# Three front stages made one, and the bf16 remainders of two attention projections formed in PSUM

## The chip, the cores and the metric

The kernel runs on one core of a Trainium2 chip. The metric is the device time of one execution in microseconds (us). A core has five engines that run side by side and meet at semaphores: TensorE (PE, matrix products into PSUM; its weight loads are listed as PEld), VectorE (DVE), ScalarE (ACT), GpSimd (POOL) and SyncE (SP, which here issues nearly all DMAs).

## The reference, cut to what matters

The reference is a stack of eleven layers on x of 2048 tokens (2 sequences of 1024) by 128 features, all in float32. The change touches the first four layers and the two attentions of the last block.

```python
x = x + 0.5 * ffn0(layernorm(x))     # the coupling net, three cycles
x = x + scan(layernorm(x))           # diagonal linear recurrence
x = x + 0.5 * ffn0(layernorm(x))     # the coupling net again
x = x + 0.5 * ffn1(layernorm(x))     # top-1 of 7 experts, and a shared expert
...
# ffn0: gf = global_net(mean over the tokens of a sequence)
for _ in range(3):
    tf = sigmoid(gelu(gelu(gelu(out @ w1) @ w2) @ w3) @ w4)
    combined = 0.7 * gf + 0.3 * tf
    out = out + (0.1 + range * (combined - 0.5) * 2) * twist(out)
# scan: h_t = A * h_(t-1) + (x_t @ B.T + b);  y = h @ C.T + c
# last block: x + attention_g(rmsnorm(x)), then x + attention_l(rmsnorm(x)),
# where q and k of each head are rotated (rope) and divided by their root mean square
```

## The kernel before

x lies in SBUF as 16 tiles of 128 tokens by 128 features; four tiles are a chunk of 512 tokens, and there are four chunks. The kernel is a row of seventeen stages. Each stage is a block with one program for each engine, written out by hand in its order, and ends in a barrier of all engines (`close` in `Core.block`, line 116).

The front is three such stages: `coupling_stage` (c1_), `scan_stage` (s_) and `coupling_stage` again (c2_). Each begins with `LayerNorm`: DVE takes the statistics of a chunk (L170, L173), GpSimd raises the variance to -0.5 (L195, L197), DVE normalises (L180), TensorE turns four tiles to features by tokens (L206) and ScalarE copies them to xnT (L212). In a coupling stage there follow three cycles. In one, TensorE's layers 1 to 4 (L438, L444, L452, L459) alternate with ScalarE's three gelus and a tanh (L506, L510, L514, L519); SP swaps the two halves of the features by DMA (L373, L374); DVE adds the base part of the output (L411), then for each chunk forms a product with the gate (L414) and adds it (L417). In the first cycle the base waits for the global net (L434, L496 to L501), and that for the sums over a sequence (L398). At the end TensorE turns the output back (L483) and DVE joins it to x (L421). The scan stage multiplies by B (L589), adds a bias on ScalarE (L575), runs the recurrence on DVE (L607) and multiplies by C (L582).

After the front stands `top1_stage` (m1_), whose argument `ahead` says how many chunks come already normalised (none here). It loads the shared expert's weights at its start (L695); TensorE turns, makes logits (L770) and runs the shared expert (L787, L792). It is called a second time later (m2_) with three chunks ahead.

`gqa_project_stage` is called for the global (gp_) and the local (lp_) attention of the last block. TensorE projects four tiles a chunk (L3198), DVE multiplies by rope's table (L3301) and sums (L3318), ScalarE squares (L3271), DVE takes means (L3322) and, after ScalarE's root (L3275), scales the heads (L3334); TensorE turns queries (L3207) and keys (L3214). Then the float32 result is split in three bf16 parts by `Split`: ScalarE rounds a part (L1517 from the remainder), DVE subtracts it from the remainder in SBUF (L1525), twice. The parts go to DRAM and come back in stacks. In the global one ScalarE also makes plain normalised rows (L3285).

## Time and profile before

| | us |
|---|---|
| median of 3 runs (lowest, highest) | 1833.39 (1831.61, 1835.34) |
| the profiled execution, whole | 1834.7 |
| its span in the profile | 1832.7 |
| PE busy | 1616.0 (88% of the span) |
| DVE busy | 1013.4 (55%) |
| ACT busy | 818.2 (45%) |
| POOL busy | 332.8 (18%) |
| mean granted clock of TensorE | 0.934 of full speed |

The span runs from the first to the last instruction of the core; the time of an execution is 2.0 us more. Busy shares are averages over all stages. The granted clock is the share of TensorE's full 2.4 GHz that it was given; 0.50 is its lower level, 1.2 GHz.

### The profile page before, as it was taken

The numbers are of one execution on the slowest core, as the hardware profiler recorded it, in microseconds if no ns is written. First come the engines' busy times: TensorE is split into PE (matmuls) and PEld (weight loads), VectorE is DVE, ScalarE is ACT, GpSimd is POOL, SyncE is SP. The second block draws the span as 40 slices with busy tenths as digits, with TensorE's granted clock in tenths as the row PEclk, the third lists the DMA queues.
The fourth block names the chain that finished last, engine by engine and source line by source line (L and its number), as shares of the span: only waits on it lengthen the run. The fifth ranks groups of instructions, "written<-read, shape, count | busy, mean of one in ns | idle before, by whom it ended". The sixth has DMA issues, their size and how long they took to land. (4 is left out here: it accounts for less than half of the span.)

```text
span 1832.7 us, 24864 instructions
## 1 busy us (share of the span) xinstructions
PE 1616.0 (88%) x8677; PEld 871.8 (48%) x8725; DVE 1013.4 (55%) x2284; ACT 818.2 (45%) x1322; POOL 332.8 (18%) x459
## 2 busy tenths in 40 slices
PE   6588985899998998899789989998599985979998
PEld 2325663344443666345544555666333333555665
DVE  6775338878784333634563353456633447964444
ACT  5253333367676323333233243222688865743221
POOL 1104331323232333300330032001000100023000
PEclk9798997799999799899899999999699987989999
DMA  4633105201000310000000005554221023204554
GB/s 104 257 69 150 54 31 144 80 28 54 28 28 2 150 54 32 14 1 1 1 1 0 1 30 121 118 118 90 65 69 33 17 46 111 69 31 106 130 113 92
DMA packets 56076, 121.00 MB, mean 66 GB/s; under 512 B 8423, under 2 KB 34695, under 8 KB 51155
## 3 DMA queue, kind: packets, MB, share of 16 engines
q1 hardware_dynamic: 53484, 114.34, 23.1%
q0 software_dynamic: 2432, 5.00, 0.8%
q8 instruction: 73, 1.20, 0.3%
q14 instruction: 48, 0.39, 0.1%
q10 hardware_dynamic: 39, 0.07, 0.0%
HBM read 86.17 MB, written 19.96 MB: 58 GB/s over the span
## 5 line engine op out<-in xcount | busy, mean ns | idle before, releaser
L2083 DVE TENSOR_REDUCE a_most<-psum 128x1 f32<-128x512 f32 (+3 forms) x304 | 181.8, 655 | 30.9 <-PE psum L1929 20.2
L2041 ACT ACTIVATE a_probs<-psum 128x512 f32<-128x512 f32 (+1 forms) x304 | 155.4, 577 | 94.8 <-PE psum L1959 62.3
L2914 ACT ACTIVATE t_silu<-psum 128x512 f32<-128x512 f32 x136 | 81.2, 597 | 241.0 <-PE psum L2972 240.0
L2989 PEld LDWEIGHTS psum<-t_slot,t_hid 128*128 128x128 f32 x1024 | 132.0, 191 | 56.7 <-issue 49.3
L2342 ACT ACTIVATE ga_probs<-psum 128x1024 f32<-128x1024 f32 (+2 forms) x160 | 138.5, 950 | 24.4 <-PE psum L2256 24.0
L3085 DVE TENSOR_TENSOR t_prod<-t_silu,psum 128x512 f32<-128x512 f32 x104 | 71.5, 688 | 137.4 <-ACT t_silu L2914 137.4
L2989 PE MATMUL psum<-t_slot,t_hid 128*128 128x128 f32 x1024 | 134.4, 276 | 3.7 <-DVE t_hid L3076 3.7
L2972 PE MATMUL psum<-xnT,t_slot 128*128 128x512 f32 x256 | 131.2, 594 | 3.1 <-ACT t_silu L2914 3.1
L2977 PE MATMUL psum<-xnT,t_slot 128*128 128x512 f32 x256 | 130.7, 592 | 0.0
L1926 PE MATMUL psum<-a_ks,a_qs 96*128 96x512 bf16 (+3 forms) x384 | 119.4, 342 | 10.8 <-DMA a_qs<-a_most_parts 3.8
L3076 DVE TENSOR_TENSOR t_hid<-t_prod,t_spread 128x512 f32<-128x512 f32 x128 | 89.5, 702 | 38.5 <-DMA t_spread<-factors 32.0
L1959 PE MATMUL psum<-a_qs,a_ks 128*128 128x512 bf16 (+3 forms) x359 | 100.5, 322 | 2.8 <-ACT a_probs L2041 2.4
L734 ACT ACTIVATE m_silu<-psum 128x512 f32<-128x512 f32 x76 | 45.2, 598 | 116.8 <-PE psum L819 71.3
L206 PE MATMUL psum<-const,xn_row 128*128 128x128 f32 x160 | 36.3, 370 | 60.4 <-DVE xn_row L180 51.0
L2278 PE MATMUL psum<-ga_probs,ga_vslot 128*32 128x512 f32 (+3 forms) x768 | 83.1, 506 | 1.6 <-DVE ga_probs L2371 0.7
L1981 PE MATMUL psum<-a_probs,a_vslot 128*32 128x512 f32 (+3 forms) x768 | 81.8, 499 | 2.6 <-POOL a_probs L1886 2.6
L1142 PE MATMUL psum<-f_apart,f_joint 128*128 128x512 f32 x192 | 83.7, 592 | 0.0
L2256 PE MATMUL psum<-ga_qs,ga_ks 128*128 128x512 bf16 (+3 forms) x361 | 78.0, 331 | 5.8 <-ACT ga_probs L2342 1.9
L2977 PEld LDWEIGHTS psum<-xnT,t_slot 128*128 128x128 f32 x256 | 48.6, 190 | 61.2 <-issue 59.3
L1926 PEld LDWEIGHTS psum<-a_ks,a_qs 96*128 96x128 bf16 x384 | 37.8, 99 | 77.4 <-issue 68.1
L2371 DVE TENSOR_TENSOR ga_probs<-ga_probs,ga_keep 128x512 f32<-128x512 f32 x64 | 43.5, 689 | 48.6 <-ACT ga_probs L2342 48.4
L212 ACT ACTIVATE xnT<-psum 128x512 f32<-128x512 f32 x40 | 23.8, 598 | 97.6 <-PE psum L206 97.3
(435 smaller groups left out, 3012.9 us busy)
## 6 DMA issues: line engine op xcount, KB each, us to landing
t_spread<-factors SPq DMA_DIRECT2D x64, 512.0 KB, 6.5
m_experts<-experts_dram SPq DMA_DIRECT2D x14, 768.0 KB, 9.9
c_halves<-xnT SPq DMA_DIRECT2D x48, 128.0 KB, 2.3
t_slot<-experts_dram SPq DMA_DIRECT2D x32, 192.0 KB, 5.4
a_qs<-scratch_q SPq DMA_DIRECT2D x16, 288.0 KB
a_ks<-scratch_k SPq DMA_DIRECT2D x24, 192.0 KB
ga_qs<-scratch_q SPq DMA_DIRECT2D x16, 288.0 KB
la_qs<-scratch_q SPq DMA_DIRECT2D x16, 288.0 KB
```

The costliest lines, as they stand in the source:

```text
L1142: ins = pe.matmul(core.psum[:, bank + j, :], lhs[:, k, j * P:(j + 1) * P], rhs(k), start=first and k == 0, stop=last and k == HALF - 1, sk ...
L1926: ins = pe.matmul(bank[:, k * wide:(k + 1) * wide], qs[0:ROWS, n % RING, qt // KPH, hh, qt % KPH * P:(qt % KPH + 1) * P], ks[0:ROWS, n % R ...
L1959: ins = pe.matmul(bank[:, i * wide:(i + 1) * wide], ks[:, n % RING, hh, kt * P:(kt + 1) * P], qs[:, n % RING, half, hh, at - half * CH:at ...
L1981: ins = pe.matmul(core.psum[32 * hh:32 * hh + 32, O_BANK[half], off:off + wide], vslot[:, n % 2, kt, hh, :], probs[:, (n * BLOCKS + b) % P ...
L2041: act.activation(probs[:, (n * BLOCKS + b) % PROBS, h0:h0 + heads, 0:wide], src, ACT.Exp, scale=SCALE).then_inc(probs_ready, 1)
L2083: v.tensor_reduce(most[:, row, h0:h0 + heads, qt % KPH], src, AX.X, ALU.max).then_inc(max_read, 1)
L2278: ins = pe.matmul(core.psum[32 * hh:32 * hh + 32, O_BANK[half], off:off + wide], vslot[:, n % 2, kt, :], probs[:, (n * BLOCKS + b) % PROBS ...
L2342: act.activation(probs[:, (n * BLOCKS + b) % PROBS, h0:h0 + heads, 0:wide], src, ACT.Exp, scale=SCALE).then_inc(probs_ready, 1)
L2972: pe.matmul(core.psum[:, g_bank(n), :], sl[:, 0, :], xc, start=True, stop=True).then_inc(gate_pe, 1)
L2977: pe.matmul(core.psum[:, u_bank(n), :], sl[:, 1, :], xc, start=True, stop=True).then_inc(up_pe, 1)
L2989: ins = pe.matmul(core.psum[:, c, t * P:(t + 1) * P], left[:, t * P:(t + 1) * P], weights, start=pair < 0 and t == 0, stop=False, skip_gro ...
L3076: v.tensor_tensor(hid[:, n % HIDS, :], prod[:, n % PRODS, :], spread[:, pair % FACTORS, c * CH:(c + 1) * CH], ALU.mult).then_inc(hid_ready, 1)
```

## The change

The front becomes one block, `front_stage`. Chunks are taken in the order 0, 2, 1, 3 (`PLACES`), so that the first two belong to different sequences. Its cycles are numbered 0 to 5, and between cycles 2 and 3 the scan's work is woven in by hand. Four `FrontNorm` objects take the place of `LayerNorm`; two of them normalise on ScalarE (with a negated mean made by two more small GpSimd steps), and the fourth normalises chunks 0 and 1 for the top1 stage, which is called with `ahead` 2. In the last cycle of each call chunks 1 and 3 are not added up on DVE: TensorE turns base and product and adds both in PSUM (`turn_base`, `turn_product`). The biases of the scan's output come from a product with a row of ones (`output_bias`). Constants and w0 are loaded in two pieces, the first of each ahead. The decay comes from a tanh in place of a sigmoid. Both top1 stages share one load of the shared expert, which SP issues in the front after the swaps of cycle 2, behind the other later loads and ahead of the clearing writes.

In both gqa stages `Split` gives way to `BankSplit`: the remainder stays in PSUM, and TensorE subtracts a part there by a bf16 product with a negated identity. Queries and keys get two banks each and are turned by products rather than transposes. The order of all engines is new. The normalised rows of the global stage are made by GpSimd, and ScalarE ends the stage with one Exp of a single column. `rope_project_stage` keeps `Split`.

```diff
+PLACES = (0, 2, 1, 3)
...
+    def pool(self, g, p):
+        k = self.k
+        a = TPC * self.places[p]
+        b = a + TPC
+        g.wait_ge(self.var_ready, TPC * (p + 1))
+        g.tensor_scalar(k.rstd[:, a:b], k.meanvar[:, a:b, 1], LN_EPS, None, ALU.add).then_inc(self.eps_added, 1)
+        if self.minus is not None:
+            g.tensor_scalar(self.minus[:, a:b], k.meanvar[:, a:b, 0], -1.0, None, ALU.mult).then_inc(self.minus_step, 1)
+        g.wait_ge(self.eps_added, p + 1)
+        g.tensor_tensor(k.rstd[:, a:b], k.rstd[:, a:b], k.mhalf[:, a:b], ALU.pow).then_inc(self.root_ready, 1)
+        if self.minus is not None:
+            g.wait_ge(self.minus_step, p + 1)
+            g.wait_ge(self.root_ready, p + 1)
+            g.tensor_tensor(self.minus[:, a:b], self.minus[:, a:b], k.rstd[:, a:b], ALU.mult).then_inc(self.rstd_ready, 1)
...
+    def scalar(self, act, p):
+        k = self.k
+        act.wait_ge(self.rstd_ready, p + 1)
+        for t in self.tiles(p):
+            act.activation(k.xn[:, t, :], k.x[:, t, :], ACT.Identity, bias=self.minus[:, t:t + 1],
+                           scale=k.rstd[:, t:t + 1]).then_inc(self.xn_ready, 1)
...
+    chunk(PLACES[0])
+    sp.dma_start(core.const[:, 0:P], dram["const"][:, 0:P]).then_inc(core.ident_in, 16)
+    chunk(PLACES[1])
+    sp.dma_start(w0[:, 0:L0_FIRST], dram["w0"][:, 0:L0_FIRST]).then_inc(w0_in, 16)
+    chunk(PLACES[2])
+    chunk(PLACES[3])
+    sp.dma_start(core.const[:, P:CONST_W], dram["const"][:, P:CONST_W]).then_inc(core.const_in, 16)
     sp.wait_ge(w0_in, 16)
     for name, rows, width, right in (("cn_w3", 64, 32, 32), ("cn_w4", 32, P, 0), ("cn_b2", 64, 1, 0), ("cn_b3", 32, 1, 0)):
         a, _ = L0_COLS[name]
         sp.dma_start(w0[rows:2 * rows, a + right:a + right + width], dram["w0"][0:rows, a:a + width],
                      allow_slow_non_contiguous=width == 1).then_inc(core.doubled, 16)
-
-
-def later_loads(core, sp, dram, loads, sorted_x, routed_y, cleared):
-
-    for tile, name, sem in loads[1:]:
+    sp.dma_start(w0[:, L0_FIRST:L0_W], dram["w0"][:, L0_FIRST:L0_W]).then_inc(w0_rest, 16)
...
+            def first_cycle(cyc):
+                base(cyc, 0)
+                base(cyc, 1)
+                base(cyc, 2)
+                product(cyc, 0)
+                product(cyc, 1)
+                output(cyc, 0)
+                output(cyc, 1)
+                base(cyc, 3)
+                product(cyc, 2)
+                output(cyc, 2)
+                product(cyc, 3)
+                output(cyc, 3)
...
+            def last_cycle(cyc):
+                for p in range(NC):
+                    base(cyc, p)
+                product(cyc, 0)
+                product(cyc, 1)
+                output(cyc, 0)
+                output(cyc, 1)
...
+            first_cycle(0)
+            middle_cycle(1)
+            last_cycle(2)
+            join(0, 0)
+            joined_statistics(0)
+            product(2, 2)
+            join(0, 1)
+            joined_statistics(1)
+            product(2, 3)
+            join(0, 2)
+            joined_statistics(2)
+            join(0, 3)
+            joined_statistics(3)
+            scan(0)
+            scan(1)
+            add_scanned(0)
+            scanned_statistics(0)
+            scan(2)
+            add_scanned(1)
+            scanned_statistics(1)
+            scan(3)
+            add_scanned(2)
+            scanned_statistics(2)
+            add_scanned(3)
+            scanned_statistics(3)
+            for p in range(NC):
+                part_sum(1, p)
+            shifts(1)
+            first_cycle(3)
+            middle_cycle(4)
+            last_cycle(5)
+            join(1, 0)
+            next_statistics(0)
+            product(5, 2)
+            product(5, 3)
+            join(1, 1)
+            join(1, 2)
+            next_statistics(1)
+            norms[3].vector(v, 0)
+            join(1, 3)
+            norms[3].vector(v, 1)
...
+            pe.wait_ge(w0_rest, 16)
+            pe.wait_ge(core.const_in, 16)
+            output_bias(0)
+            turn_base(2, 2)
+            layer4(2, 1)
+            turn_output(2, 0)
+            turn_output(2, 1)
+            turn_base(2, 3)
+            output_bias(1)
+            turn_product(2, 2)
+            norms[1].turn(pe, 0, SCAN_BANK[0])
+            turn_product(2, 3)
+            input_product(0)
+            norms[1].turn(pe, 1, SCAN_BANK[1])
+            input_product(1)
+            norms[1].turn(pe, 2, SCAN_BANK[2])
+            output_product(0)
+            input_product(2)
+            norms[1].turn(pe, 3, SCAN_BANK[3])
+            output_product(1)
+            input_product(3)
+            output_bias(2)
+            output_product(2)
+            output_bias(3)
+            norms[2].turn(pe, 0, 0)
+            output_product(3)
+            norms[2].turn(pe, 1, 1)
+            layer1(3, 0)
+            layer1(3, 1)
...
+            cycle(1)
+            cycle(2)
+            norms[1].scalar(act, 0)
+            norms[1].copy(act, 0, SCAN_BANK[0])
+            norms[1].scalar(act, 1)
+            input_bias(0)
+            norms[1].copy(act, 1, SCAN_BANK[1])
+            norms[1].scalar(act, 2)
+            input_bias(1)
+            norms[1].copy(act, 2, SCAN_BANK[2])
+            norms[1].scalar(act, 3)
+            input_bias(2)
+            norms[1].copy(act, 3, SCAN_BANK[3])
+            input_bias(3)
+            norms[2].scalar(act, 0)
+            norms[2].copy(act, 0, 0)
+            norms[2].scalar(act, 1)
+            norms[2].copy(act, 1, 1)
+            norms[2].scalar(act, 2)
+            gelu1(3, 0)
+            norms[2].copy(act, 2, 2)
+            norms[2].scalar(act, 3)
+            gelu1(3, 1)
+            norms[2].copy(act, 3, 3)
+            head(3)
...
+    def part(self, act, step, p, i):
+        if p == 0:
+            act.wait_ge(self.heads_pe[i], step + 1)
+            if step >= 2:
+                act.wait_ge(self.spilled[i][step % 2], 16 * (self.PARTS, self.pair)[i] * (step // 2))
+        else:
+            act.wait_ge(self.rest_pe[i], (self.PARTS - 1) * step + p)
+        act.activation(self.parts[i][:, p, step % 2, :], self.banks[i][step % 2], ACT.Copy).then_inc(self.part_ready[i], 1)
+
+    def subtract(self, pe, step, p, i):
+        n = self.banks[i][step % 2].shape[0]
+        pe.wait_ge(self.part_ready[i], self.PARTS * step + p)
+        pe.matmul(self.banks[i][step % 2], self.minus[0:n, 0:n], self.parts[i][:, p - 1, step % 2, :], start=False, stop=True,
+                  skip_group_check=True).then_inc(self.rest_pe[i], 1)
...
-                g.tensor_tensor(shift[:, :], core.meanvar[:, :, 0], rise[:, :], ALU.mult).then_inc(rise_step, 1)
-                g.wait_ge(rise_step, 3)
-                g.tensor_scalar(shift[:, :], shift[:, :], -1.0, None, ALU.mult).then_inc(rise_step, 1)
+                for t in range(NT):
+                    g.tensor_scalar(core.xn[:, t, :], core.x[:, t, :], core.meanvar[:, t, 0:1], rise[:, t:t + 1], ALU.subtract, ALU.mult).then_inc(row_made, 1)
...
+            project(1)
             ln.tensor(pe, 3)
-            project(1)
-            for c in range(NC):
-                if c + 2 < NC:
-                    project(c + 2)
-                turn(c)
+            project(2)
+            project_tile(3 * TPC)
+            turn(0)
+            project_tile(3 * TPC + 1)
+            subtract(0, 1)
+            project_tile(3 * TPC + 2)
+            subtract(0, 2)
+            project_tile(3 * TPC + 3)
+            turn(1)
+            for c in range(1, NC - 1):
+                subtract(c, 1)
+                subtract(c, 2)
+                turn(c + 1)
...
+            ln.scalar(act, 0, gain=gain)
+            ln.scalar(act, 1, gain=gain)
+            ln.scalar(act, 2, gain=gain)
+            all_values(0)
+            squares(0)
+            all_values(1)
+            ln.scalar(act, 3, gain=gain)
+            roots(0)
+            squares(1)
+            all_values(2)
+            roots(1)
+            part(0, 0)
+            squares(2)
+            roots(2)
+            part(0, 1)
+            part(0, 2)
+            part(1, 0)
+            part(1, 1)
+            part(1, 2)
+            all_values(3)
+            squares(3)
+            part(2, 0)
+            roots(3)
+            part(2, 1)
+            part(2, 2)
+            act.activation(early[:, :], core.zero[:, 0:1], ACT.Exp)
...
+            both_products(0)
+            join(0)
+            both_products(1)
+            means(0)
+            join(1)
+            both_products(2)
+            scale(0)
+            means(1)
+            join(2)
+            scale(1)
+            means(2)
+            scale(2)
+            both_products(3)
+            join(3)
+            means(3)
+            scale(3)
...
-        coupling_stage(core, w0, w0_in, "c1_", (lambda sp: (first_loads(core, sp, dram, loads), second_copies(core, sp, dram, w0, w0_in)), lambda sp: later_loads(core, sp, dram, loads, sorted_x, routed_y, cleared)))
-        scan_stage(core, w0, "s_")
-        coupling_stage(core, w0, w0_in, "c2_")
-
-        top1_stage(core, 0, w1, w1_in, dram["experts1"], sorted_x[0], routed_y[0], cleared, scattered, returned, 0, "m1_")
...
+            front_stage(core, w0, w0_in, w0_rest, lambda sp: first_loads(core, sp, dram, w0, w0_in, w0_rest),
+                        lambda sp: later_loads(core, sp, dram, loads, sorted_x, routed_y, cleared, shared_load), "c_")
+            top1_stage(core, 2, w1, w1_in, dram["experts1"], shared, shared_in, sorted_x[0], routed_y[0], cleared, scattered, returned, 0, "m1_")
```

## Rows read from the trace of the kernel before

**Rows 1.** Busy time by stage (stretch, length, engines, PEclk, DMA share, GB/s)

```profile
0.00:61.06 61.06, 39.62 (x122) 14.02 (x122) 40.95 (x102) 28.79 (x46) 5.39 (x13) 0.97 0.54 160
61.06:87.16 26.10, 17.61 (x56) 10.86 (x56) 19.70 (x63) 6.59 (x10) 5.07 (x8) 0.60 0.65 260
1273.89:1320.90 47.01, 26.42 (x99) 16.55 (x99) 35.03 (x96) 27.92 (x57) 8.70 (x13) 0.71 0.31 82
1498.85:1542.30 43.45, 25.32 (x96) 16.29 (x96) 28.60 (x60) 21.00 (x36) 1.67 (x4) 0.74 0.40 102
```

**Rows 2.** Timeline of the first cycle (start, us, engine, line, operation, out<-in, idle)

```profile
15.44 3.51 PE L438 MATMUL psum<-xnT,w 128*128 128x512 f32 x6
...
24.95 2.74 DVE L411 SCALAR_TENSOR_TENSOR xnT<-c_halves,c_shift,xnT 128x512 f32<-128x512 f32 x4
...
27.61 0.75 DVE L414 SCALAR_TENSOR_TENSOR c_prod<-c_gate,c_slope,c_halves 128x512 f32<-128x512 f32 x1
```

**Rows 3.** Timeline of the last cycle, the scan stage and the second coupling stage

```profile
50.48 0.75 DVE L414 SCALAR_TENSOR_TENSOR c_prod<-c_gate,c_slope,c_halves 128x512 f32<-128x512 f32 x1 [0.88 <-ACT c_gate L519]
...
51.65 1.13 PE L459 MATMUL psum<-c_hid,w 32*128 32x512 f32 x4 [0.91 <-ACT c_hid L514]
...
62.62 1.04 POOL L197 TENSOR_TENSOR rstd<-rstd,mhalf 128x4 f32<-128x4 f32 x1
...
65.45 0.60 ACT L212 ACTIVATE xnT<-psum 128x512 f32<-128x512 f32 x1 [2.93 <-PE psum L206]
...
69.71 2.07 PE L589 MATMUL psum<-xnT,w 128*128 128x512 f32 x2 [0.69 <-ACT xnT L212]
...
71.76 1.23 DVE L607 TENSOR_TENSOR_SCAN s_h<-s_decays,s_bx 128x512 f32<-128x512 f32 x1
...
75.44 0.69 ACT L575 ACTIVATE s_bx<-psum,w 128x512 f32<-128x512 f32 x1 [2.16 <-PE psum L589]
...
109.37 0.75 DVE L414 SCALAR_TENSOR_TENSOR c_prod<-c_gate,c_slope,c_halves 128x512 f32<-128x512 f32 x1
```

**Rows 4.** Timeline of the start of the two top1 stages

```profile
141.55 0.87 DVE L170 BATCH_NORM_STATS2 stats<-x 128x6 f32<-128x128 f32 x4 [0.86 <-PEq L116]
...
144.75 1.15 PE L206 MATMUL psum<-const,xn_row 128*128 128x128 f32 x4 [5.73 <-DVE xn_row L180]
...
146.72 1.24 PE L206 MATMUL psum<-const,xn_row 128*128 128x128 f32 x4 [0.82 <-DVE xn_row L180]
...
153.86 1.27 POOL L713 TENSOR_TENSOR m_hid<-m_silu,m_upper 128x512 f32<-128x512 f32 x1 [3.93 <-ACT m_upper L737]
...
604.86 2.07 PE L787 MATMUL psum<-xnT,m_shared 128*128 128x512 f32 x2 [1.49 <-DMA m_shared<-experts_dram]
```

**Rows 5.** Timeline of the gqa projection stages and what follows the first

```profile
1290.34 1.63 ACT L3285 ACTIVATE xn_row<-x,gp_shift,gp_rise 128x128 f32<-128x128 f32 x4
...
1296.27 0.68 DVE L1525 TENSOR_TENSOR gp_rest<-psum,ga_parts 128x512 f32<-128x512 f32 x1
...
1298.37 0.82 DVE L3334 TENSOR_TENSOR gp_heads<-gp_heads,gp_root 128x640 f32<-128x640 f32 x1
...
1317.09 1.12 PE L3207 MATMUL psum<-const,gp_heads 128*128 128x128 f32 x4 [5.60 <-DVE gp_heads L3334]
...
1318.13 1.92 PE L3214 MATMUL psum<-const,gp_heads 128*32 128x128 f32 x8
...
1322.00 1.28 ACT L2342 ACT_TABLE_LOAD   x1
...
1539.32 1.91 PE L3214 MATMUL psum<-const,lp_heads 128*32 128x128 f32 x8
```

**Rows 6.** Busy time and granted clock in three short stretches

```profile
64.00:76.00 12.00, 9.77 (x22) 4.89 (x22) 9.60 (x36) 3.73 (x6) 3.54 (x5) 0.50 1.03 417
...
1293.00:1296.00 3.00, 1.13 (x10) 0.79 (x8) 2.39 (x5) 2.11 (x4) 0.00 (x0) 1.00 0.00 0
...
1296.00:1300.00 4.00, 3.82 (x8) 2.27 (x9) 3.86 (x9) 1.06 (x4) 0.00 (x0) 0.62 0.19 66
```

700 lines of the change are left out of this document (421 added, 279 removed).

## The prediction

> **What bounds the kernel now.** I read the page first: TensorE is busy for 88% of the span, but that is an average over seventeen stages, and the change touches four of them. So I asked for the busy time of each engine stage by stage. The first coupling stage and the scan stage after it show no engine that works all the time: in 61 us DVE is busy 41, ACT 29; in the 26 us of the scan stage DVE 20 and ACT 7, and the two gqa projection stages have 35 and 29 us of DVE in 47 and 43 [rows 1]. These stages are chains of hand-overs between engines. There the timeline is the view to read, since it shows the order on each engine and what ended each wait.
>
> In the timeline of the front the reader is to see four losses. The first cycle's four base additions hold DVE for 2.74 us, and product 0 follows at 27.61 with no idle time before it: DVE itself was late [rows 2]. Between stages all engines stop: DVE waits 0.86 us at a barrier [rows 4], and ScalarE loads tables as it does at 1322.00, 1.28 us each [rows 5]. The second stage's norm cannot start before all four chunks have left the first. And TensorE's granted clock is 0.50 of full speed, the 1.2 GHz level, from 64 to 76 us [rows 6], so that a 128x512 product takes 2.07 us where it takes 1.13 at the 2.4 GHz level [rows 3].
>
> **The change, part by part.** I scheduled the new order by hand with the durations of the rows. I keep the clock of the old trace in each part, so a number can be compared with the old row.
>
> *Start.* Only the identity (64 of 272 KB of constants) and 340 of 533 KB of w0 lie ahead of x. I put the second chunk at 5.4 us and the fourth at 8.4. The norms then end about a microsecond earlier, but TensorE is slow until 17 us (six instructions in 3.51 us [rows 2]), and its order now has layer1(0) and layer1(1) ahead of the last two turnings. I get the fourth chunk copied at 16.6. After that the global net's layers no longer stand behind each other's waits and no table load stands in the way: shift at 22.0, bases 0 to 2 by 24.1 (0.66 us each, four took 2.74), product 0 at 24.2 where it was at 27.61 [rows 2]. Gain **3.4**. With TensorE fast at once it would be 5.3; with every TensorE step there slow, 2.
>
> *First-cycle order.* Two products ahead of two outputs give output 1 some 0.25 us early, but base 3 now stands ahead of output 2, and layer1(2) stands ahead of layer2(0) on TensorE. That costs 0.4 in cycle 0 and again in cycle 3: **-0.8**.
>
> *From cycle 2 to cycle 3*, the largest term. Product 0 of cycle 2 starts at 50.48 as before. TensorE does the bias row and turn_base ahead of layer4, which now ends near 53.3, where it ended at 52.8 (51.65 plus 1.13 [rows 3]); join 0 ends at 54.5, its statistics (0.87 and 0.3 more) at 55.7. GpSimd's power takes 1.04 [rows 3], with three small steps 2.1: ScalarE may start at 57.85. From here ScalarE sets the pace. Four normalised tiles take 1.63 (the same operation with two pointers [rows 5]), the copy 0.60 and the bias 0.69 [rows 3], so 2.9 a chunk; with the wait for the first turning and for the last product, the fourth bias ends at 71.0. The scans (1.23 each [rows 3]), joins and statistics of DVE fit between. Then norm 2: four times 2.23, two gelus of 0.69, one wait of a microsecond: the fourth chunk is copied at 82.75. Sum, global net (again without a load), shift and three bases take 6.65, as counted at the start: product 0 of cycle 3 at 89.4. It was at 109.37 [rows 3]. Gain **20.0**. The new swaps queue on SP behind the later loads, now with the shared expert's 768 KB; the DMA engines are full until 76 [rows 6], the swap is issued at 74.4 and base 0 wants it at 86.7, so that wait is covered by 9 us.
>
> This holds if TensorE stays at its higher level. It fell here after it had stood nearly idle in the old kernel. In the gqa stage it stayed at 1.00 through three microseconds with 1.13 us of work and fell in the next four [rows 6]. New work for it between 52 and 83 is 60 to 85% of the time, so I take the high level as likelier, not as sure. [...] The slow work between 58 and the last copy is some 34 us (eight turnings of 1.24 [rows 4], fourteen products of about 1.75, that is 2.07 less what overlaps), against 25 available, of which a part would come back as unbroken work brings the clock up: **+5 to +9**.
>
> The Trainium skill ("TensorE: Matmul & The Clock Gate", "Seeing it yourself") says the lower level is what an idle engine falls back to; the fall after the old stage's end agrees. By it alone the sum would stay as it is, since there is no idle stretch left.
>
> *Hand-over to the top1 stage.* The front's DVE ends some 2.6 us later against its last cycle, because it takes the statistics (1.15) and norms (1.1) of two chunks along and gives two outputs to TensorE; but TensorE's first turning, which came 3.2 us after DVE's start, comes at once (144.1 against 144.75), the second chunk's at 145.2 against 146.72 [rows 4], and everything after is one chain of TensorE. Gain **1.5**. In the second top1 stage TensorE no longer waits 1.49 us for the shared weights [rows 4]: **1.5**.
>
> *The two gqa projection stages.* Eight subtractions of 0.68 [rows 5] leave DVE, and become bf16 matmuls of some 0.5 us on TensorE; ScalarE loses sixteen normalised tiles (6.5 us, in the first of the two). The query turning grows from four to eight instructions, as the key turning has (1.92 us slow, half that fast): +0.7 at the slow level. Against that the first chunk is scaled later, because chunk 1 and 2 stand before it: its turning starts at 1295.1. DVE then runs means 1 (1.05), join 2 (0.8), scale 1 (2.3, of which the last step is 0.82 [rows 5]), means 2, a root and scale 2, 7.8 in all: 1302.8; part(1,2) of ScalarE ends at 1306.9 with TensorE fast and at 1309.6 with it slow; squares, means, root and scale of chunk 3 follow; and the last turning (3.7, always slow, as 1317.09 to 1320.05 was [rows 5]) ends at 1316.2 or 1318.9. The old end was 1320.05. So +3.8 or +1.2, middle **2.5**. The second stage, which had no rows to make (it took 43.45 against 47.01 [rows 1]), by the same steps ends at 1539.5 or 1542.2, old 1541.23: +1.7 or -1.0, middle **0.4**. Exp's table is loaded in both stages under the last turning rather than at 1322.00 [rows 5], ahead of the first scores. That is worth between nothing and 1.28 each; TensorE's scores take most of a microsecond less than the load, so I take 1.0 each: **2.0**. If that cover were gone, it would be 0. The key parts end earlier too, so the first stack's loads keep up with the shorter stage.
>
> Sum: 3.4 - 0.8 + 20.0 + 1.5 + 1.5 + 2.5 + 0.4 + 2.0 = 30.5. The profiled execution took 1834.7 us (its span 1832.7 and 2.0 around it), so it would take 1804.2. The median of the three runs shown, 1833.39, is 1.3 below it. Prediction: **1803 us**.
>
> **A rule against it.** GpSimd now makes sixteen 128x128 tiles from 1285.5 on. 512 columns cost it 1.27 us [rows 4], so a tile some 0.32 to 0.5, 5 to 8 us in all, while DVE joins and scales. Above I let them run side by side. If each DVE instruction there had to wait for one tile, ten of them would add 3 to 5 us to the first gqa stage. The Trainium skill ("SBUF — State Buffer", "SBUF: two separate sides") states such a rule: DVE with two operands in SBUF and GpSimd lock each other out of a shared pair of ports for a whole instruction. No row here shows both busy long enough to tell. By the one reading the sum is 30.5, by the other 26.5, that is 1807 us.
>
> **Rivals.**
> 1. TensorE falls to the lower level in the middle of the front. For it: the scan stage ran so, at 0.60 on average [rows 1]. Against: no barrier, no idle stretch. Price 5 to 9: 1808 to 1812 us. Chance 0.25.
> 2. DVE waits for GpSimd in the first gqa stage: 1807 us. Chance 0.08.
> 3. More than forecast: TensorE fast from the first cycle (+1.9) and through both gqa stages (+2.6), top1 warm sooner (+1): 1797 us or a little less. Chance 0.1.
> 4. Slower than before. One mechanism: the front never gets TensorE to its higher level. A cycle has ten product slots of 0.85 us fast and twice that slow, 17 us against the 11.4 of a cycle (50.48 less 27.61, for two [rows 2, 3]): 5.6 a cycle in six cycles, 34 us, and 9 in the middle, 43 in all: 1846 us. It decides from five slow cycles. Against it: the first coupling stage ran at 0.97 of full speed [rows 1]. Chance 0.02.
> 5. No change within 0.2% (about what a measurement of this kernel can tell from none): most of the mid-front gain would have to fail. Chance 0.02.
> The forecast itself, 1797 to 1808 us, has 0.53.
>
> **Range and chances.** The hand schedule leaves out small hand-overs, so I stretch the upper side beyond rival 1, and the lower to just below rival 3: 1794 to 1815 us. Faster 0.96, same 0.02, slower 0.02.
>
> **What would show it.** Product 0 of cycle 0 near 24 us; from product 0 of cycle 2 to that of cycle 3 some 39 us rather than 58.9; the top1 stage's first turning near 121.5 us, with no statistics of chunks 0 and 1 behind it; granted clock near 1.00 in the middle of the front; one table load before the top1 stage's; the first gqa stage 43 to 46 us long, the second 42 to 44. Wrong would be a fall to 0.50 there, ScalarE waiting for turnings, or a gqa stage that ends later than now.

## The result, and the profile after

| | us |
|---|---|
| predicted, with its range | 1803.0 (1794 to 1815) |
| median of 4 runs (lowest, highest) | 1804.63 (1803.04, 1806.09) |
| the kernel before on the same occasion, 4 runs | 1832.91 (1831.61, 1835.34) |
| ratio, 95% interval | 0.9844 (0.9827 to 0.9861) |
| the profiled execution, whole; its span | 1805.04; 1803.3 |

The changed kernel is 1.6% faster, by 28 us, where 30.5 were forecast. The time was right to within 2 us; that says little on its own, because several terms of the sum were wrong in both directions. The timeline of the changed kernel has the rows that answer to [rows 2], [rows 3] and [rows 4]:

```profile
24.56 1.41 DVE L529 SCALAR_TENSOR_TENSOR c_prod<-c_gate,c_slope,c_halves 128x512 f32<-128x512 f32 x2
...
47.72 1.42 DVE L529 SCALAR_TENSOR_TENSOR c_prod<-c_gate,c_slope,c_halves 128x512 f32<-128x512 f32 x2 [1.04 <-ACT c_gate L838]
...
56.08 1.65 ACT L323 ACTIVATE xn_row<-x,c_n_minus,rstd 128x128 f32<-128x128 f32 x4 [3.62 <-POOL c_n_minus L309]
...
80.77 0.59 ACT L336 ACTIVATE xnT<-psum 128x512 f32<-128x512 f32 x1
...
89.68 1.41 DVE L529 SCALAR_TENSOR_TENSOR c_prod<-c_gate,c_slope,c_halves 128x512 f32<-128x512 f32 x2
...
125.65 1.84 PE L205 MATMUL psum<-const,xn_row 128*128 128x128 f32 x8 [5.17 <-PEq L118]
```

Product 0 of cycle 0 is at 24.56 (forecast 24.2), and product 0 of cycle 3 comes 41.96 us after that of cycle 2 (forecast 39, before 58.9). The top1 stage's first turning is at 125.65, where 121.5 was forecast, and it comes after 5.17 us in which TensorE stood idle. The end of the first gqa stage, ahead of [rows 5] by 21.5 us through what came before it:

```profile
1290.43 1.28 ACT L3667 ACT_TABLE_LOAD   x1
...
1291.28 1.16 PE L3555 MATMUL psum<-const,gp_heads 128*128 128x128 f32 x8 [1.50 <-DVE gp_heads L3709]
...
1292.37 1.06 PE L3561 MATMUL psum<-const,gp_heads 128*32 128x128 f32 x8
1292.44 2.17 SPq L1718 DMA_DIRECT2D scratch_q<-ga_parts  x3
1295.85 1.07 ACT L1764 ACTIVATE ga_parts<-psum 128x512 bf16<-128x512 f32 x2 [3.91 <-PEq L118]
...
1296.82 1.01 ACT L2686 ACTIVATE ga_probs<-psum 128x1024 f32<-128x1024 f32 x1
```

The stage begins at 1252.38 and ends at 1295.85: 43.5 us, where [rows 1] has 47.01. The last turning takes 2.15 us, not the 3.7 forecast for the slow level, and what ends the stage is no longer TensorE (1293.43) but SP, whose last issue ends at 1294.61. The busy time by stretch shows the clock. The columns are those of [rows 1].

```profile
125.65:132.40 6.75, 6.75 (x20) 4.54 (x21) 4.41 (x24) 3.07 (x4) 2.53 (x4) 0.51 0.86 319
132.40:145.00 12.60, 12.60 (x55) 7.53 (x54) 1.54 (x5) 6.95 (x12) 5.99 (x5) 0.99 0.64 267
...
61.00:81.00 20.00, 17.10 (x77) 9.49 (x75) 14.65 (x51) 16.34 (x37) 10.97 (x20) 1.00 0.95 369
81.30:84.80 3.50, 3.50 (x11) 1.47 (x10) 0.69 (x1) 1.57 (x4) 0.00 (x0) 0.51 0.34 75
```

In the front's middle TensorE mostly has its higher level, as forecast, but not throughout: it falls from 57.5 to 60.9 and from 81.4 to 84.8 (the second stretch is shown). After the front it runs nearly 7 us of unbroken work at the lower level.

The largest stretch, from product 0 of cycle 2 to that of cycle 3, before and after:

```profile
50.48:109.37 58.89, 37.23 (x125) 19.77 (x126) 42.33 (x136) 19.51 (x32) 10.14 (x16) 0.71 0.55 207
...
47.72:89.68 41.96, 37.60 (x157) 19.85 (x156) 27.98 (x91) 27.45 (x60) 16.77 (x32) 0.92 0.80 306
```

TensorE is busy as long as before (37.2 and 37.6 us), DVE gives up 14 us, and the granted clock is 0.92 on average instead of 0.71. How much of the gain is the clock and how much the barriers, the table loads and the work taken from DVE, no run separates.

Where the 29.4 us between the two spans came from, stretch by stretch:

| stretch | forecast | profile |
|---|---|---|
| up to product 0 of cycle 0 | 3.4 | 3.05 |
| product 0 to 2 cycles later, both calls | -0.8 | -0.56 |
| product 0 of cycle 2 to that of cycle 3 | 20.0 | 16.93 |
| product 0 of cycle 5 to the end of the top1 stage | 1.5 | 1.30 |
| the rope projection and attention stages, unchanged | 0 | -1.54 |
| second top1 stage and what follows up to the first gqa stage | 1.5 | 2.33 |
| first gqa stage, up to the first scores' Exp | 3.5 | 4.97 |
| the rest of the global attention, unchanged | 0 | 0.36 |
| second gqa stage, up to the first scores' Exp | 1.4 | 3.34 |
| the rest, unchanged | 0 | -0.78 |
| sum | 30.5 | 29.40 |

The middle of the front gave 3.1 less than forecast and the gqa stages 3.4 more.

### The profile page after: what moved, and what is told of

It is laid out like the page before. It is cut to its first block and busy times, and to the rows that moved or that the text cites. A ratio compares the mean times of both kernels' runs of the same rounds, so it can differ in the third digit from the quotient of the medians.

```text
span 1803.3 us, 24998 instructions
## 1 busy us (share of the span) xinstructions
PE 1626.4 (90%) x8783; PEld 881.5 (49%) x8833; DVE 990.0 (55%) x2226; ACT 818.6 (45%) x1338; POOL 355.4 (20%) x491
## 3 DMA queue, kind: packets, MB, share of 16 engines
q1 hardware_dynamic: 53628, 113.55, 23.2%
## 5 line engine op out<-in xcount | busy, mean ns | idle before, releaser
L2427 DVE TENSOR_REDUCE a_most<-psum 128x1 f32<-128x512 f32 (+3 forms) x304 | 181.9, 655 | 32.3 <-PE psum L2273 20.2
L2715 DVE TENSOR_TENSOR ga_probs<-ga_probs,ga_keep 128x512 f32<-128x512 f32 x64 | 43.5, 689 | 48.9 <-ACT ga_probs L2686 48.6
L2230 POOL TENSOR_SCALAR_AFFINE_SELECT a_probs<-a_probs 128x512 f32<-128x512 f32 x64 | 40.5, 633 | 145.0 <-ACT a_probs L2385 144.8
L1020 POOL DMA_INDIRECT routed_y<-m_outs,m_token x44 | 42.1, 958 | 113.9 <-DVE m_outs L1272 94.6
```

The lines of the kernel that those rows point to most:

```text
L2427: v.tensor_reduce(most[:, row, h0:h0 + heads, qt % KPH], src, AX.X, ALU.max).then_inc(max_read, 1)
```

## The experiments

Each kernel below is the changed kernel with one edit. Medians are over 4 or 5 runs, ratios are against the kernel before, timed beside it. A single median moves by 2 us and more between occasions, so each experiment is also read in its profile. The names of the runs are only labels.

**The gqa stage of before put back.** The whole function `gqa_project_stage` is that of the kernel before (too long to print).

> The changed kernel with the gqa projection stage of the kernel before put back whole (remainders on DVE, transposes, rows on ScalarE, no early Exp); the front and the two top1 stages stay as changed. By the terms of my sum the two gqa stages with the early Exp were worth 2.5 + 0.4 + 2.0 = 4.9 us, so this would take about 1809.5. By the profile after they gave more: 4.97 us up to the first scores of the global attention and 3.3 up to those of the local one, 8.3 together, so about 1812.9. Rival, that the two parts are not independent (run variation of the attention stages carries the difference): anywhere between 1807 and 1815 with the first gqa stage still 47.0 us long. Decided on the stage lengths: 47.0 and 43.5 us if the stage behaves as in the kernel before.

It took 1812.39 us (1807.69 to 1813.93), ratio 0.9871 (0.9853 to 0.9888). The stages were 47.25 and 43.54 us long, as before, and their first Exp of scores came 49.63 and 45.92 us after their start, against 44.44 and 42.51 with the change: 5.2 and 3.4, 8.6 us together. So by the profiles the gqa part is worth 8 to 9 us, not the 4.9 of the sum. The totals don't decide between the two: the medians are 7.8 us apart, but on different occasions, and the ratios differ by 0.0027, that is 4.9 us. What this run has over the kernel before, 0.9871 of its time or some 24 us, is the front and the shared weights.

**Without the early Exp.**

```diff
-            act.activation(early[:, :], core.zero[:, 0:1], ACT.Exp)
```

> The changed kernel without the single-column Exp at the end of the gqa stages. My sum: 1.0 us lost in each, 1806.6. Rival A, full price of a table load on the path: 1.28 each, 1807.2. Rival B, the load is hidden behind the first scores: nothing, 1804.6. Rival C, ScalarE's load at the end of the stage costs something itself because it stands where the barrier is waited for: a gain. In the profile: from the release of the barrier to the first Exp of scores 0.97 us now, 2.2 to 2.4 without; stage ends unchanged, if SP and not ScalarE ends them.

1806.84 us (1802.08 to 1809.16), ratio 0.9849 (0.9831 to 0.9867): the total can't tell. ScalarE's timeline of this kernel can:

```profile
1292.30 1.07 ACT L1764 ACTIVATE ga_parts<-psum 128x512 bf16<-128x512 f32 x2 [5.49 <-PEq L118]
1293.39 1.28 ACT L2686 ACT_TABLE_LOAD   x1
1294.68 1.02 ACT L2686 ACTIVATE ga_probs<-psum 128x1024 f32<-128x1024 f32 x1
```

The first scores' Exp starts 2.38 us after the release instead of 0.97, in both attentions: 1.41 each. The whole load lay on the path, and a little of the hand-over with it; my 1.0 each, for which I let the scores cover part, was too small. The stages were 43.4 and 40.6 us long, within what the executions with the early Exp have (41.7 to 44.2, and 40.6 to 41.7), and ScalarE's last work came 3 to 4 us ahead of TensorE's: it ends neither.

**More work for TensorE in the middle of the front.**

```diff
+            def fill(n, bank):
+                for i in range(n):
+                    pe.transpose(core.psum[:, bank, i % TPC * P:(i % TPC + 1) * P], core.c("ident"), core.c("ident"))
...
+            fill(8, 2)
             norms[1].turn(pe, 0, SCAN_BANK[0])
...
+            fill(8, 4)
             norms[2].turn(pe, 3, 3)
```

> The changed kernel with eight more 128x128 transposes of the identity (results unused) on TensorE at each of two places where it stood idle for 1.1 us: ahead of the first turning of the scan's norm, and ahead of the last turning of the second coupling's. Theory: the two falls of the granted clock (57.8 to 60.9 and 81.4 to 84.9 us) follow these idle stretches, and cost the 1.7 us by which the way from the fourth copy to product 0 of cycle 3 was over the forecast, and some 0.4 in the scan. Then product 0 of cycle 3 is at 87.6 to 88.0 instead of 89.7, and the time near 1802.8. Rival, the falls have another cause (the idle stretches before the barrier, or the share of work over a longer time): the clock falls all the same, product 0 at 89.7 or up to 0.5 later for the work added.

1802.76 us (1801.25 to 1804.01), ratio 0.9826 (0.9812 to 0.9839). Neither fall came at its old place, but one came at 70.2 to 73.6, where it costs less. From product 0 of cycle 2 to that of cycle 3 it was 40.13 us, and product 0 of cycle 3 stood at 86.01. The top1 stage began at 121.99, 3.65 us ahead of the changed kernel's profile, and still ended at 259.80, where that had ended at 259.95. TensorE's slow stretch in it had grown from 7.0 to 13.1 us.

Of the theory this shows half. In all ten executions without extra work TensorE stood idle for 1.1 us or more ahead of the first turning, and a fall came 9.8 to 11.0 us after product 0 of cycle 2 (7.0 in the run with the outputs on DVE, further down); with the extra work it did not come here, and also not in the next run that has it. The price is small: 40.13 here against 40.35 to 40.69 in the seven executions with the same orders, that fall and none at 81. The fall at 81.4 proves nothing, since only the changed kernel's execution had it, though the idle stretch of 1.1 us ahead of it is in all ten. And the fall at 70.2, here and in six executions without extra work, has no idle stretch of more than 0.4 us in the 8 us ahead of it. The total is not apart from the changed kernel's (0.9839 and 0.9827 overlap); in the profile the gain was given back behind the front.

**The first stack's key loads issued by GpSimd.**

```diff
-        self.stacks.load(sp, 0)
+        self.stacks.load(sp, 0, keys=False)
...
+    def pool_keys(self, g):
+        self.stacks.landed(g, NC // NB)
+        self.stacks.load(g, 0, queries=False)
```

> The changed kernel with the three key loads of the first stack of each gqa stage issued by GpSimd instead of SP. Theory: the end of both gqa stages is now set by SP's queue (its last issue ends at 1294.6 and 1512.3 us, TensorE's last product at 1293.4 and 1511.9), so that three issues less bring the release 1.5 us and some 0.6 us earlier: the stages 42.0 and 41.0 us long instead of 43.5 and 41.6, the time near 1802.5. Rival: the barrier waits for something else, or GpSimd takes as long for the issues: lengths unchanged, 1804.6, or later.

1807.95 us (1807.10 to 1809.43), ratio 0.9858 (0.9843 to 0.9873). The first gqa stage was 45.1 us long, longer than with SP:

```profile
1289.05 1.91 POOL L1744 DMA_DIRECT2D ga_ks<-scratch_k  x3 [11.75 <-DMA scratch_k<-ga_parts]
...
1291.10 1.06 PE L3571 MATMUL psum<-const,gp_heads 128*32 128x128 f32 x8
1295.89 0.52 POOL L2578 MEMSET ga_vslot<- 128x512 f32 x1 [4.93 <-POOLq L118]
```

GpSimd's issues end at 1290.96 and TensorE's products at 1292.16, yet the engines drain for the barrier only at 1295.3. In the second stage GpSimd's issues end at 1508.79 and the drain comes at 1513.1: 4.3 us later in both; the second stage was 41.7 us long, as before. The rival won. What holds the barrier is GpSimd's own drain, the instruction with which an engine waits for its work to finish: it took 5.06 and 5.02 us here, and 4.5 us behind GpSimd's issues in the top1 stages (in the kernel before, the changed one and this one), where most of its other drains took 1.1. The run doesn't yet say whether SP ended the stage before.

**Work for TensorE at the start and the end of the front too.**

```diff
+            pe.wait_ge(core.zero_set, 1)
+            for i in range(3):
+                pe.matmul(core.psum[:, 5, :], core.zero[:, 0:P], core.zero[:, 0:CH], start=True, stop=True)
             pe.wait_ge(core.ident_in, 16)
...
             turn_product(5, 3)
+            fill(30, 2)
```

> The changed kernel with the sixteen extra transposes in the middle of the front (as in the run before with extra work there), 30 more at the front's end, while DVE still joins and normalises, and three 128x512 products of zeros at the start, before x has arrived. Theory: after the front TensorE stands idle for 5 us, its clock falls, and the top1 stage's first 6.8 to 13.3 us run at 0.50; that took back all that the middle had gained. If it is kept busy up to the barrier, the top1 stage starts at 0.9 to 1.00 and is 3 to 6 us shorter, p1's start at 254 to 256 us instead of 259.4 to 260; product 0 of cycle 0 is at 22.7 or before; the time near 1797. Rival: the clock falls at the barrier all the same (1.5 us of idleness are enough), then p1 starts at 257 to 260 and the time is 1801 to 1803. Second rival: the top1 stage's end is set by something that does not move with its start (a transfer), then p1's start stays at 259.6 though the clock is high.

1794.47 us (1791.60 to 1795.88), ratio 0.9786 (0.9771 to 0.9801): faster than the changed kernel beyond both intervals. Its windows and timeline around the end of the front:

```profile
50.00:84.00 34.00, 31.39 (x146) 16.71 (x144) 23.73 (x85) 24.22 (x54) 17.76 (x32) 1.00 0.82 307
...
104.00:120.95 16.95, 13.77 (x88) 9.20 (x87) 12.36 (x36) 5.32 (x9) 3.29 (x4) 1.00 0.06 14
120.95:122.00 1.05, 1.05 (x8) 0.83 (x8) 1.05 (x8) 0.38 (x1) 0.00 (x0) 1.00 0.32 35
122.00:128.60 6.60, 6.35 (x19) 4.16 (x18) 3.37 (x18) 3.18 (x5) 2.60 (x5) 0.50 0.98 377
```

```profile
115.61 3.44 PE L757 MATMUL psum<-const 128*128 128x128 f32 x30
120.95 1.06 PE L205 MATMUL psum<-const,xn_row 128*128 128x128 f32 x8 [1.91 <-PEq L118]
```

The middle now has no fall at all (1.00 from 50 to 84; 39.78 us from product 0 to product 0), and product 0 of cycle 0 is at 22.06: with the products of zeros TensorE reached its higher level at 6.0 us. The top1 stage starts at the higher level, loses it 1.05 us later all the same and runs 6.6 us at 0.50. It ends at 255.52, where the next stage, p1 of the expectation, starts. The first rival was right on the barrier: 1.91 us without work were followed by a fall. (The 30 extra instructions ahead of it were transposes; no run tried products there.) The gain came all the same: 4.7 us from the front against the changed kernel's profile. Another 4.7 us came from stages behind top1 that the edit doesn't touch, 3.1 of them in the second top1 stage.

**The writes of chunk 2 issued after the barrier.**

```diff
     def sync(self, sp):
+        for c in self.stacks.owed:
+            self.stacks.spill(sp, c, None)
...
-        for c in range(half, NC - 1):
-            self.stacks.spill(sp, c, self.part_ready)
```

> The changed kernel with the three writes of chunk 2's query parts to DRAM taken out of the gqa projection stages and issued by SP at the start of the attention stage that follows. Theory: SP's queue ends both gqa stages (its last issue lies 1.2 and 0.4 us behind TensorE's last product, and the barrier follows an issue by 0.65 us, a product by 0.3): the stages become 1.5 and 0.8 us shorter, 42.0 and 40.8 us; with the writes off the path the time is 1802.3. Rival: the stack loads of the attention stages come later by the 1.85 us of the three issues and TensorE waits for them there: nothing gained, 1804.6.

1801.89 us (1799.09 to 1809.00), ratio 0.9843 (0.9822 to 0.9864). TensorE's end and the release in the first gqa stage:

```profile
1289.04 1.92 PE L3564 MATMUL psum<-const,gp_heads 128*32 128x128 f32 x8
1291.79 3.34 SPq L1720 DMA_DIRECT2D scratch_q<-ga_parts  x5
...
1291.82 1.07 ACT L1766 ACTIVATE ga_parts<-psum 128x512 bf16<-128x512 f32 x2 [4.14 <-PEq L118]
```

The release now follows TensorE's last product by 0.86 and 0.84 us in the two stages, where it followed by 2.42 and 1.64 in the changed kernel. So SP's queue had ended the first stage, at a cost of 1.6 us: all eight executions with the writes in place show 2.1 to 2.8 us there (the ones with keys by GpSimd and with rows on ScalarE apart). The second it had ended only sometimes: four executions with the writes in place have 0.82 or 0.83 too, so the writes cost between nothing and 0.8 there. The total doesn't show it: in this execution TensorE's last turning ran at the lower level and took 3.93 us, and the first stage was 43.95 us long.

**The rows on ScalarE again.**

```diff
-                for t in range(NT):
-                    g.tensor_scalar(core.xn[:, t, :], core.x[:, t, :], core.meanvar[:, t, 0:1], rise[:, t:t + 1], ALU.subtract, ALU.mult).then_inc(row_made, 1)
...
+                    for t in range(TPC * c, TPC * (c + 1)):
+                        act.activation(core.xn[:, t, :], core.x[:, t, :], ACT.Identity, bias=shift[:, t:t + 1], scale=rise[:, t:t + 1]).then_inc(row_made, 1)
```

> The changed kernel with the sixteen normalised rows of the first gqa stage made by ScalarE again, four after each root, GpSimd making only their scale and offset. My sum took 6.5 us from ScalarE for this, of which the part on the path had to be small, since DVE's chain is as long: the stage 1.5 to 4 us longer, 45 to 47.5 us, 1806 to 1808.6. Rival A, ScalarE is the pace everywhere: 6.5 longer, 50.0. Rival B, GpSimd's rows slow DVE by a shared port: the stage gets shorter or stays at 43.5 us, and DVE's operations beside the rows (0.91 and 1.05 us now against 0.82) are quicker.

1808.17 us (1804.71 to 1809.01), ratio 0.9860 (0.9843 to 0.9877). TensorE's last product came 45.4 us after the start instead of 41.1, and the stage was 46.3 us long instead of 43.5. Groups of DVE and GpSimd from 1260 to 1279 and the single times of GpSimd's tiles (shortest, median and longest, in ns), in the changed kernel first:

```profile
L3695 DVE TENSOR_TENSOR gp_heads<-gp_both 128x640 f32<-128x640 f32 x3 | 2.5, 848 | 0.0
...
L3709 DVE TENSOR_TENSOR gp_heads<-gp_heads,gp_root 128x640 f32<-128x640 f32 x2 | 1.9, 936 | 0.1
...
L3520 POOL TENSOR_SCALAR xn_row<-x,meanvar,gp_rise 128x128 f32<-128x128 f32 x16 | 14.5, 920 | 0.1
...
L3520 POOL TENSOR_SCALAR xn_row<-x,meanvar,gp_rise x16: 787/802/1475, 1264.1 to 1277.2; 128x128 f32<-128x128 f32 x16
```

and in the kernel with the rows on ScalarE:

```profile
L3707 DVE TENSOR_TENSOR gp_heads<-gp_both 128x640 f32<-128x640 f32 x3 | 2.5, 819 | 0.0
L3721 DVE TENSOR_TENSOR gp_heads<-gp_heads,gp_root 128x640 f32<-128x640 f32 x2 | 1.6, 824 | 0.1
```

DVE's operations on two operands in SBUF take 848 and 936 ns beside GpSimd's tiles and 819 and 824 without: 0.3 us in all. The one that pays is GpSimd. Its tiles take 0.79 us where no such operation of DVE runs, and 1.01 to 1.48 in the five during which one of about 0.8 us ends (the longest, from 1277.19, has the whole of DVE's L3709 at 1277.25 inside it); over the sixteen tiles this is 2.1 us. DVE's operations that read PSUM (L3683) keep their 0.82 us. So the two do get in each other's way, but it lay off the path.

Of the 4.4 us by which TensorE's last product came later, 2.6 are the longer chain (DVE's last scaling 41.5 us after the start instead of 38.9); the other 1.8 are the last turning, which ran at the lower level here and took 3.93 us instead of 2.15. The stage itself grew by only 2.8, because in the changed kernel SP and not TensorE ends it.

**The last cycle's outputs all on DVE.**

```diff
             product(2, 2)
+            output(2, 2)
...
-            turn_base(2, 2)
             layer4(2, 1)
...
-            turn_product(2, 2)
+            turn_output(2, 2)
```

(and so for chunk 3, and in cycle 5.)

> The changed kernel with the outputs of chunks 1 and 3 in the last cycles added up by DVE and turned by transposes, as those of the other two. TensorE loses four instructions a chunk, DVE gains 0.69 us a chunk. Theory: DVE sets the pace there, so each of the two ends of a call is 0.7 to 1.4 us later: from product 0 of cycle 2 to that of cycle 3 41.2 to 41.9 us instead of 40.4, m1 0.7 to 1.4 later; 1806 to 1807.4. Rival: ScalarE's tiles set the pace and cover it: no change, 40.4.

1800.95 us (1798.49 to 1801.44), ratio 0.9828 (0.9813 to 0.9843): neither theory nor rival had it faster. It was split: from product 0 of cycle 5 to the top1 stage 14.22 us instead of 12.81, 1.4 more as expected; but from product 0 of cycle 2 to that of cycle 3 39.79 instead of the 40.4 of its neighbours. TensorE's timelines of two executions with product 0 of cycle 2 at 45.91 and 45.94, first with TensorE adding,

```profile
47.14 1.16 PE L729 MATMUL psum<-const,xnT 128*128 128x128 f32 x8
48.23 1.13 PE L679 MATMUL psum<-c_hid,w 32*128 32x512 f32 x4
...
54.82 1.48 PE L330 MATMUL psum<-const,xn_row 128*128 128x128 f32 x4 [1.11 <-ACT xn_row L323]
```

then with DVE adding:

```profile
47.10 1.13 PE L683 MATMUL psum<-c_hid,w 32*128 32x512 f32 x4
...
54.17 1.63 PE L330 MATMUL psum<-const,xn_row 128*128 128x128 f32 x4 [1.30 <-ACT xn_row L323]
```

The turning of the base holds layer 4 up by 1.13 us, and of that 0.65 reaches the first turning of the scan's norm.

**All that gained, together.** Extra work at all three places, the writes of chunk 2 after the barrier, and DVE's outputs in the middle only (no code beyond the diffs above).

> The changed kernel with what gained so far put together: the extra work on TensorE at the start, in the middle and at the end of the front; the writes of chunk 2's query parts issued in the following attention stage; and, in the middle of the front only, the outputs of chunks 1 and 3 added by DVE (that run had 39.8 us from product 0 of cycle 2 to that of cycle 3 where its neighbours had 40.4, but lost 1.4 us at the front's end, where PSUM adds here). Theory, the parts add up: the kernel with extra work alone took 1794.5; less 1.6 and 0.8 for SP's queue and 0.3 to 0.6 in the middle, 1791.6. Rival: the parts touch the same wait, or the order moves the moments of low clock elsewhere: 1793 to 1796.

1794.51 us (1790.42 to 1796.11), ratio 0.9776 (0.9763 to 0.9790). It beats the kernel before and the changed one, and can't be told from the kernel with extra work alone: the rival's range was met, not the theory. The middle took 39.80 us as with extra work alone (39.78), so DVE's outputs add nothing on top of it; TensorE stands idle for 1.9 us at their place, ahead of the extra work, and a fall of 6.8 us follows. The first gqa stage was 42.5 us long, but its first scores came no sooner:

```profile
1287.30 1.07 ACT L1776 ACTIVATE ga_parts<-psum 128x512 bf16<-128x512 f32 x2 [2.79 <-PEq L118]
...
1288.37 2.53 PE L2613 MATMUL psum<-ga_qs,ga_ks 128*128 128x512 bf16 x8 [2.35 <-DMA ga_ks<-scratch_k]
```

TensorE now waits for the first stack's keys, which land at 1288.37. With the barrier earlier the load is late next, and 1.69 us pass between release and first Exp instead of 0.97.

**Nothing normalised ahead for the top1 stage.**

```diff
-            next_statistics(0)
...
-            next_statistics(1)
-            norms[3].vector(v, 0)
             join(1, 3)
-            norms[3].vector(v, 1)
...
-            top1_stage(core, 2, w1, ...
+            top1_stage(core, 0, w1, ...
```

> The changed kernel with nothing normalised ahead for the first top1 stage: the front's DVE ends after its last join, and the top1 stage takes the statistics and norms of all four chunks itself, as in the kernel before. My sum gave the hand-over 1.5 us: from product 0 of cycle 5 to the release into the next stage after top1 the changed kernel would take 1.5 us less than this one, at the same length of low clock in the top1 stage; 1806.1. Rival, the norms taken ahead only move work across the barrier: equal. Second rival: the longer idle stretch of TensorE that the norms ahead bring (5.2 us) costs more clock than they save: this one is faster.

1803.84 us (1802.76 to 1805.36), ratio 0.9835 (0.9820 to 0.9850): no slower. From product 0 of cycle 5 to the end of the top1 stage it took 149.98 us, with 14.0 us of slow work; executions of the changed order with 12.4 to 13.1 us of slow work took 149.9 to 150.6. No gain from the norms taken ahead shows.

**The shared expert loaded again.**

```diff
+            if call:
+                sp.dma_start(shared[:, :], dram_experts[7].rearrange("p j d -> p (j d)")).then_inc(shared_in, 16)
```

> The changed kernel with the shared expert's weights loaded once more at the start of the second top1 stage, ahead of the routed experts'. My sum: 1.5 us lost in the second top1 stage, where TensorE would wait for them again; 1806.1. Rival: the wait is covered by the turning of the chunks, nothing lost; or more, 1.9 us, as the profiles of before and after differ there.

1806.06 us (1802.87 to 1808.12), ratio 0.9842 (0.9827 to 0.9857): the total can't tell. In the profile the first product with the shared weights starts 4.17 us after the release and waits for them:

```profile
587.50 2.08 PE L1083 MATMUL psum<-xnT,m_shared 128*128 128x512 f32 x2 [0.52 <-DMA m_shared<-experts_dram]
```

It started 5.14 us after the release in the kernel before [rows 4] and 3.50 in the changed one. One load is worth 0.7 to 1.6 us at this place. The stage's length doesn't show it: 131.0 us here, and 128.9 to 133.2 in the executions with one load.

**The old order of the first cycle.**

```diff
-                product(cyc, 0)
-                product(cyc, 1)
-                output(cyc, 0)
-                output(cyc, 1)
                 base(cyc, 3)
+                for p in range(NC):
+                    product(cyc, p)
+                    output(cyc, p)
```

> The changed kernel with DVE's order of the kernel before in the first cycle of each call: all four bases, then product and output of each chunk in turn. My sum charged the new order with 0.4 us a call (-0.8 in all): then this kernel is 0.8 us faster, product 0 of cycle 1 some 11.3 to 11.4 us behind that of cycle 0 (11.65 in the changed kernel, 11.38 in the one before) though product 0 of cycle 0 comes 0.7 later. Rival: base 3 waits for ScalarE's and TensorE's late fourth chunk, and holds product 0 up by more than it saves: 0.5 to 1 us slower a call.

1806.75 us (1801.94 to 1813.41), ratio 0.9849 (0.9824 to 0.9875). From product 0 of cycle 0 to that of cycle 1 it was 11.37 us instead of 11.65, from the shift to product 0 2.92 instead of 2.25. The new order costs 0.3 a call behind product 0 and saves 0.7 ahead of it, so it gains 0.4. The expectation counted only the part behind product 0 in its total of -0.8. The total is too spread to tell.

## Why the prediction came out right

The profiles of the fourteen executions, in us. "Slow work" is the time from the top1 stage's first turning to the return of the higher level, read in windows of 1 us; the last column is from product 0 of cycle 5 to the end of the top1 stage.

| kernel | product 0, cycle 0 | product 0, cycle 2 to 3 | slow work in top1 | to top1's end |
|---|---|---|---|---|
| before | 27.61 | 58.89 | 8.8 | 148.42 |
| changed | 24.56 | 41.96 | 7.0 | 147.12 |
| old gqa stage | 24.62 | 40.56 | 8.8 | 148.09 |
| no early Exp | 24.21 | 40.42 | 8.6 | 148.39 |
| extra work, middle | 22.73 | 40.13 | 13.1 | 150.63 |
| keys by GpSimd | 22.74 | 40.45 | 12.5 | 150.17 |
| extra work, all | 22.06 | 39.78 | 7.9 | 147.39 |
| writes later | 22.76 | 40.35 | 6.3 | 146.90 |
| rows on ScalarE | 24.85 | 40.69 | 12.4 | 149.86 |
| outputs on DVE | 22.79 | 39.79 | 8.4 | 149.07 |
| all together | 21.81 | 39.80 | 7.9 | 147.37 |
| nothing ahead | 22.93 | 40.62 | 14.0 | 149.98 |
| shared again | 23.21 | 40.59 | 12.6 | 150.64 |
| old first order | 25.19 | 41.25 | 8.8 | 147.91 |

**Start, 3.4.** Right, and so were its bounds (2 and 5.3): 2.8 to 4.9 in the executions with the same front, 3.05 in the profiled one. Two groups make up the spread: TensorE reached its higher level at 16.3 to 17.6 us in four executions (product 0 at 24.2 to 24.9) and at 11.9 to 12.7 in six (22.7 to 23.2). With products of zeros ahead it was 6.0 and 5.8 us, and product 0 came at 22.06 and 21.81.

**First-cycle order, -0.8.** The size was off: -0.56 behind the two product 0.

**The middle, 20.0.** The mechanism was right (ScalarE paces it at 2.6 to 2.9 us a chunk), the term was too large. Counted from product 0 of cycle 2 I had ScalarE's first tile at 7.4, the fourth bias done at 20.5, the fourth copy at 32.3, product 0 of cycle 3 at 38.9. The changed kernel has 8.4, 21.9, 33.6 and 42.0; the execution with the later writes 8.4, 21.8, 33.6 and 40.4. So 1.0 is lost ahead of ScalarE's first tile in every execution that keeps this order: the bias row and the turning of the base occupy TensorE from 47.90 to 50.04, 2.1 us ahead of layer 4, and I had charged them 0.5. The run with the outputs on DVE shows it, since it got 0.65 of this back. Another 0.4 goes in the hand-overs that the schedule left out. The last 1.6 were the second fall of the clock, from 81.4 to 84.8, under the global net; only this one of the executions had it there, and of the other twelve with the new front eleven had 6.7 us from the fourth copy to product 0, as forecast (the twelfth, with the old first cycle, 7.4). So without this fall the term is 18.2 to 18.5. The first rival, a fall in the middle at +5 to +9, was right that it falls and wrong in its size: the falls were 3.4 us long (6.8 in two executions), not the whole middle, and the level came back while TensorE worked. No run shows a price of 5 to 9: the fall near 57 cost 0.2 to 0.6 us, the one at 81 cost 1.6. One reading of the sum was also loose: its 1.13 us for a product at the higher level is layer 4, four instructions on 32 rows; two instructions of 128x512, the 2.07 of the scan, take 1.12 in the changed kernel, so the number stands.

**The Trainium skill** ("TensorE: Matmul & The Clock Gate", "Seeing it yourself") shows the lower level as what follows a stretch without products. The fall at 57.5, 0.9 us behind a stretch of 1.1 us without one, agrees, and the extra work there took it away; the prediction had seen no idle stretch left in the middle, and there were two of 1.1 us. The fall at 81.4 came 2.1 us behind the second although TensorE had worked for 17.1 of the 20 us up to 81; the falls at 70 to 72 in seven other executions had no such stretch near. Those the runs leave without a cause.

**The hand-over, 1.5.** The number came out (1.30) by luck. Where nothing was taken ahead, nothing was lost. With the same slow work as the kernel before (8.6 to 8.8 us), the changed order took 147.9 to 148.4 us against 148.42: 0 to 0.5 us, not 1.5. The profiled execution has 7.0. What moves this stretch by 3.7 us is how long TensorE's work at the lower level lasts after the idle end of the front: 146.9 to 147.4 us with 6.3 to 7.9 of slow work, 149.9 to 150.6 with 12.4 to 13.1. That the front's end idles 5.2 us, and what this costs behind it, stands nowhere in my sum; the step assumed "one chain of TensorE" at a clock of its own.

**Shared weights, 1.5.** Right on the wait: the first shared product starts 1.6 us sooner after the release, of which the run with a second load gave back 0.7. That the stage ended sooner for it is not shown.

**The gqa stages, 2.5 and 0.4.** Too small: 3.55 and 1.93. I took the middle between the chain with TensorE fast and slow, and let the last turning be slow always. The chain came out at the fast end: DVE's last scaling reached the turning 38.9 and 36.2 us after the start, where I had 38.6 and 37.0 for the fast case, and the turning of the first stage took 2.15 us, not 3.7. That would have given 5.1 us in the first stage. The missing 1.6 is SP, as the run with the later writes shows: its three writes of chunk 2 stand behind the five loads of the first stack, and the barrier waits for them. I had not looked at SP's queue there, though the same five loads and three writes stood there in the kernel before, and ended 0.1 us ahead of TensorE's last product in its second stage.

**Exp's table, 2.0.** 2.8; the load lay on the path whole.

**GpSimd's lock, 3 to 5 (the second rival).** 0.3 us on DVE. The Trainium skill ("SBUF — State Buffer", "SBUF: two separate sides") has whichever of DVE, with both inputs in SBUF, and GpSimd comes second wait for the whole instruction of the other; here such DVE operations took 0.03 and 0.11 us longer on average, and GpSimd's tiles 0.2 to 0.7 us longer where one ended in them. So there is a wait, it fell mostly on GpSimd, and the price on DVE was wrong. The prediction also had a tile at 0.32 to 0.5 us, a share of a 512-column operation; it takes 0.79 alone.

**What stays open.** Stages with the same code in all the executions with the new front (but for the second load in one) differed by more than single terms of the sum: the second top1 stage and the two stages behind it took 320.2 to 326.1 us together. Slow work at the start of that top1 stage lasted 6.5 us with all together, 8.7 with the writes later and 12.9 in the changed kernel. So some 5 of the 10 us by which the kernel with extra work beats the changed one in all its runs are not accounted for by its front. No run tells whether the moments are chance or follow from when the stage starts. Nor does one split the 17 us of the front's middle.

## What to carry to other kernels

An idle stretch of TensorE can cost more behind it than in it: after 2 to 5 us at a stage's end 6 to 14 us of the next stage ran at the lower level here, where work takes about twice as long. Price what stands behind an idle stretch too. Where it can't be scheduled away, instructions whose results nobody uses may be worth trying (the two kernels that had them at all three places were the two fastest; half of their 10 us is explained). A time forecast for one stage should be compared at equal clock before it is called right. Where a stage is a chain ending in a barrier, count every queue up to the barrier, the one that only issues DMAs too, and then ask for the load behind it: taking the wait from SP made the stack's load the next. A step that gives work to an idle engine still has a place in that engine's order, and what stands behind it there pays.
